# Graph network with two message-passing layers: in the fused stage, ScalarE takes the edge network's output behind the selectors and one-hots of a step

## The reference

```
h = relu(layernorm(x))
Q, K, V = h@Wq, h@Wk, h@Wv                          # 8 heads of 32
score[e] = (Q[dst[e]] . K[src[e]]) / sqrt(32)  +  relu(edge_attr[e]1000.00:1200.00 200.00, 195.33 (x1252) 118.17 (x1251) 188.28 (x352) 185.10 (x462) 156.62 (x145) 1.00 0.84 245 + b1) @ W2 + b2     # per head
alpha = softmax of score over the edges of each dst
x = x + (segment_sum(alpha * V[src], dst) @ Wo + bo)
h = relu(layernorm(x))
x = x + relu(segment_sum(norm * sigmoid(h@gate[rel]) * (h@weight[rel])[src], dst))
```

## Time and profile before

| | |
|---|---|
| time, median of 3 runs | 5421.86 us (5421.21 to 5422.06) |
| profiled execution | 5423.78 us, of which 5422.0 from the first to the last instruction |
| busy over the span | PE 86%, PEld 50%, DVE 61%, ACT 61%, POOL 62% |
| the page's slices in which TensorE is at 8 or 9 tenths and ScalarE at 9 | from the third to the 18th of 40, 135.6 us each: most of the fused stage |

### The profile page before, as it was taken

How to read it: one execution, slowest core, us unless ns; L and a number is a source line. 1 busy time by engine, 2 the same in 40 slices (tenths; PEclk the granted TensorE clock), 3 DMA queues, 4 the chain that set the end, 5 groups by cost and what they waited for, 6 DMA issues and landing times. The chain is left out here.

```text
span 5422.0 us, 89845 instructions
## 1 busy us (share of the span) xinstructions
PE 4659.5 (86%) x20748; PEld 2708.1 (50%) x20749; DVE 3311.3 (61%) x7106; ACT 3304.8 (61%) x7926; POOL 3379.6 (62%) x3364
## 2 busy tenths in 40 slices
PE   8899999999999999998899999777777777676766
PEld 5455555555555555554444444344444444444443
DVE  6489999999999999999633333333333333333334
ACT  3499999999999999997544444333333333333333
POOL 0277777777777777777200000477777777777776
PEclk9899999999999999999999999766666667777677
DMA  4588888888888888887444443333333333333334
GB/s 140 157 247 244 242 243 243 240 245 241 245 242 242 244 243 245 242 241 225 133 140 143 141 140 140 123 105 106 105 105 105 105 106 105 105 105 105 105 105 142
DMA packets 542017, 932.63 MB, mean 172 GB/s; under 512 B 102705, under 2 KB 351631, under 8 KB 541712
## 3 DMA queue, kind: packets, MB, share of 16 engines
q0 software_dynamic: 208384, 648.75, 40.9%
q1 hardware_dynamic: 333328, 280.23, 16.9%
HBM read 795.82 MB, written 132.87 MB: 171 GB/s over the span
## 5 line engine op out<-in xcount | busy, mean ns | idle before, releaser
L1033 POOL DMA_INDIRECT kv_rows<-kv_d,idx x1664 | 1790.3, 1076 | 550.0 <-issue 395.0
L1828 PE MATMUL m_sums<-m_rows,m_oh 128*128 x3328 | 1389.7, 566 | 589.6 <-ACT m_rows L1808 514.8
L1765 POOL DMA_INDIRECT m_rows<-msg_d,m_idx x1568 | 1486.5, 948 | 507.4 <-issue 472.8
L1808 ACT ACTIVATE m_rows<-m_rows,m_norm 128x256 f32<-128x256 f32 x1568 | 710.8, 500 | 1267.0 <-DMA m_rows<-msg_d,m_idx 1267.0
L1828 PEld LDWEIGHTS m_sums<-m_rows,m_oh 128*128 128x128 f32 x3328 | 836.6, 275 | 1142.9 <-issue 1019.9
L1850 DVE TENSOR_TENSOR agg<-agg,m_sums 128x256 f32 x832 | 350.3, 421 | 1296.1 <-PE m_sums L1828 1292.5
L1226 PE MATMUL sums<-kv_rows,onehot 128*128 128x264 f32 x3328 | 942.3, 406 | 29.1 <-issue 20.9
L1226 PEld LDWEIGHTS sums<-kv_rows,onehot 128*128 128x128 f32 x3328 | 565.9, 190 | 467.5 <-issue 260.3
L1698 PE MATMUL p_m<-wr,h1T 128*128 128x512 f32 x1568 | 710.8, 596 | 0.0
L1183 PE MATMUL p_q<-shelf,pickT 128*128 x4992 | 688.4, 274 | 21.3 <-ACT pickT L1090 10.1
L1279 DVE TENSOR_TENSOR prod<-p_q,kv_rows 128x512 f32<-128x512 f32 x832 | 566.8, 681 | 54.6 <-DMA kv_rows<-kv_d,idx 30.7
(11 more groups left out here) (194 smaller groups left out, 4003.2 us busy)
## 6 DMA issues: line engine op xcount, KB each, us to landing
msg_d<-msg SPq DMA_DIRECT2D x196, 512.0 KB
dsts<-dstrow_d SPq DMA_DIRECT2D x208, 256.0 KB
ef_raw<-in_edge_attr_dram SPq DMA_DIRECT2D x195, 256.0 KB
kv_rows<-kv_d,idx POOLq DMA_INDIRECT x1664, 4.2
m_rows<-msg_d,m_idx POOLq DMA_INDIRECT x1568, 2.7
kv_d<-kvo SPq DMA_DIRECT2D x49, 260.0 KB, 2.1
pens<-pens_d SPq DMA_DIRECT2D x52, 192.5 KB
emlp<-mlp_d SPq DMA_DIRECT2D x52, 128.0 KB
```

The source lines that it names most:

```text
L1033: pool.indirect_dma_start(rows[:, lane, k, a:a + KV], None, kv_d[:, :], bass.IndirectOffsetOnAxis(idx[:, half, c:c + 1], 0)).then_inc(gath ...
L1765: pool.indirect_dma_start(rows[:, u, k, :], None, msg_d[:, :], bass.IndirectOffsetOnAxis(idx[:, u // HALF, c:c + 1], 0)).then_inc(gathered ...
L1808: last = nc.scalar.activation(rows[:, u, k, :], rows[:, u, k, :], ACT.Copy, scale=norm[:, bass.ds(2 * g + k, 1)])
L1828: last = nc.tensor.matmul(sums[u % BANKS][:, 0:D], onehot[:, u % HOTS, k, :], rows[:, bass.ds(slot, 1), k, :].rearrange("p a d -> p (a d)" ...
```

## The change

Two calls of ScalarE's turn move: `pick` and `hot` stand ahead of the takes of the edge network, where they stood behind them. Nothing is added and nothing is removed.

```diff
                     if is_step(s - LATE):
                         measure_dst(s - LATE)
+                    if is_step(s + 3):
+                        pick(s + 3, (u + 3) % PICKS)
+                    if is_step(s - LATE):
+                        hot(s - LATE, (u - LATE) % HOTS2)
                     if u % U == 0 and is_quad(m + 1):
                         take_ef(m + 1)
                     if u % U == 0 and is_quad(m):
...
                     if u % U == 3 and is_quad(m + 1):
                         take_hidden(m + 1, 1)
-                    if is_step(s + 3):
-                        pick(s + 3, (u + 3) % PICKS)
-                    if is_step(s - LATE):
-                        hot(s - LATE, (u - LATE) % HOTS2)
                     if u % R == 5 and is_chunk(c):
                         weights(c, (u // R - 1) % 2)
```

## The result

The changed kernel takes 5869.21 us (median of 4 runs, 5867.51 to 5872.41) against 5421.96 us for the kernel before (4 runs): 1.0824 times the time before, with a 95% interval of 1.0812 to 1.0837. Its profiled execution took 5872.41 us, 448.6 more than that of before.

What follows compares the result with a forecast made beforehand. The prediction took TensorE to bound the fused stage. Stalls of 9.37 us a chunk over 47.25 chunks, 442.7 us, plus one take of 1.2, made 444 us more: 5866 us, range 5800 to 5945, forecast chance 84%.

Steps and rivals of the forecast that it cites:

- TensorE sets the pace: Fused stage: TensorE is busy 195.3 of 200 us, and any wait put in front of it costs its full length.
- The selectors cost nothing: Moved `pick` calls: their wait is long met and TensorE needs them three turns later, so no cost.
- The one-hot starts at S + 0.26 and lets ScalarE go 0.41 later: S is the start of a TensorE turn's select; the one-hot starts 0.26 us after it, releasing ScalarE 0.41 us later.
- Turns of class 3, 1.99: Turns numbered 3 mod 4: output layer starts 1.99 us after the select's start, not 0.75; 1.24 us more.
- Turns of class 1, 1.99: Turns numbered 1 mod 4: output layer starts 1.99 us after the select's start, not 0.75; 1.24 us more.
- Class 0, 1.32: Turns numbered 0 mod 4: hidden matmuls start 1.32 us after the select's start, not 0.75; 0.57 us more.
- The softmax's turns hide it: Softmax work in a chunk's turns hides stalls: turn 0 costs nothing, turn 5 0.08 us, turn 4 gains 0.53.
- Class 2 stays at 2.80: Turns numbered 2 mod 4 have no take and stay at 2.80 us.
- ScalarE is ready in time: ScalarE's heaviest stretch ends at most 3.8 us after the select's start; next one-hot due at 3.81; no cost.
- The sum: A chunk of 16 turns grows by 9.37 us, 45.98 to 55.35; over 47.25 chunks 442.7 us; total 5866.
- Rivals: One-hots come sooner, 5294 us (3%); TensorE catches up, 5755 (6%); clock falls, 6211 (4%); no effect, 5422 (3%).

## Why the prediction was right, point by point

- *TensorE sets the pace*: right. Every stall put in front of it came out in the total.
- *The selectors cost nothing*: right, 5420.74 us with them alone. They are needed two turns later, though, and not three: `pick(t+3)` is used by `select(t+3)`, in TensorE's turn t+2.
- *The one-hot starts at S + 0.26 and lets ScalarE go 0.41 later*: right, 0.26 and 0.42 (1013.46, 1013.72, 1014.14).
- *Turns of class 3, 1.99*: 1.98 (1013.46 to 1015.44).
- *Turns of class 1, 1.99*: mis-sized, 2.07 (1020.75 to 1022.82), and 2.07 in turn 5 as well (1007.03 to 1009.10). 0.08 in four turns of a chunk is 15 us more. The row that I took, 1.32 us from take to output layer, was one of a class 3 turn; class 1 takes 1.39 (1021.43 to 1022.82), and did so before (246.38 to 247.77).
- *Class 0, 1.32*: 1.30 (1017.40 to 1018.70).
- *The softmax's turns hide it*: right. They are four of a chunk's 16 (0, 2, 4 and 5), and not five. Turn 0 still 1.63 (1044.83 to 1046.46); turn 4 fell to 1.31 (1003.67 to 1004.98), and TensorE no longer waited for VectorE there (L1207, 0.0).
- *Class 2 stays at 2.80*: 2.80 (1010.66 to 1013.46).
- *ScalarE is ready in time*: right, but with little to spare. Behind turn 5, with the softmax's `weights` in it, ScalarE still waits 0.26 us for the sum (1010.92); before the one-hot at 1013.72 it waits 0.91.
- *The sum*: 55.35 us forecast for a chunk, 55.42 measured; 5866 for 5869. Some of this closeness is luck. The error in class 1, 0.32 a chunk, is met by small ones the other way: classes 0 and 3 give back 0.08 together, and 0.14 us of turn 3 that the forecast had left out went too (2.84 us from 1017.62 to 1020.46 before, where such a turn takes 2.70 from 1005.90 to 1008.60). What held turn 3 up by 0.14 isn't shown: the trace names no releaser there.
- *Rivals*: the time excludes them all, and the run with four buffers in the old order excludes that one-hots were ever TensorE's time. The granted clock of the window stayed at 1.00, though TensorE was idle for 1.16 us of a 3.94 us turn (1013.46 to 1017.40), and as long in about half of the turns. The Trainium skill (TensorE: Matmul & The Clock Gate, section "A second HAM failure mode: psum-queue depth-cycling") says that frequent brief idling can make the clock swing; this trace shows no such swing.

The rows of the kernel before for class 1 and turn 3:

```profile
246.38 1.25 ACT L1067 ACTIVATE hid<-p_hid,b1s 128x512 f32<-128x512 f32 x2
...
247.77 0.64 PE L1172 MATMUL p_mlp<-hid,w2s 128*32 128x256 f32 x8 [0.72 <-ACT hid L1067]
...
1017.62 0.82 PE L1183 MATMUL p_q<-shelf,pickT 128*128 x6
```

## What to carry to other kernels

An engine that takes its instructions in order, as ScalarE does here, passes on every wait to all that stands behind it: before moving an instruction forward, look at what it waits for and at what another engine needs from the instructions that it now precedes. Put the instruction whose input comes last at the end of the turn, or give it a buffer more: here either makes 433 us or more of difference. The stalls in front of the engine that sets the pace could be priced here from starts in the trace of the kernel before, to within 1% of the loss (444 us for 447); the one delay that was taken from another kind of turn is the one that was off.

## What the runs showed that I had not expected

TensorE starts the first half of the output layer 0.15 us after the take's end (1021.43 plus 1.24, to 1022.82 in the changed kernel's timeline), the second half 0.05 us after it (1014.14 plus 1.25, to 1015.44). The first half waits on two semaphores and the second on one; whether that is the cause wasn't tried. And freeing the engine that sets the pace of 1.2 us of waits a chunk gave back a third of them: the second wait only moved, and turns 7 and 9 grew. VectorE is busy there for 189 us of 200; that it sets the pace of these turns is argued, not shown.
